# A graph-network kernel in three passes: the weight matrix of each source block built by a product, stored in pass 0 and read back in pass 1

## The reference

```python
src, dst = cat(src, arange(n)), cat(dst, arange(n))      # with self-loops
deg  = segment_sum(ew, dst);  dinv = rsqrt(deg)
conv = segment_sum((h @ W)[src] * (dinv[src] * ew * dinv[dst]), dst) + b
x = layernorm(x + sigmoid(conv(relu(conv(x, W1, b1)), W2, b2)))
z = x @ fc_w.T;  rh = edge_attr @ fc_r_w.T
e = leaky_relu(z[src] @ a0 + z[dst] @ a1 + rh @ a2)
alpha = softmax of e over the edges of one dst
x = layernorm(x + relu(segment_sum(alpha * (z[src] + rh), dst) + z @ loop_w))
```

## Time and profile before

| | us |
|---|---|
| median of three timed runs | 2405.95 |
| lowest and highest | 2403.78, 2406.47 |
| the profiled execution, first to last instruction | 3348.6 |
| PE busy | 2044.2 (61%) |
| DVE busy | 1834.8 (55%) |
| POOL busy | 1718.9 (51%) |
| ACT busy | 946.7 (28%) |

### The profile page before, as it was taken

How to read it: one execution, slowest core, us unless ns; L and a number is a source line. 1 busy time by engine, 2 the same in 40 slices (tenths; PEclk the granted TensorE clock), 3 DMA queues, 4 the chain that set the end, 5 groups by cost and what they waited for, 6 DMA issues and landing times.

```text
span 3348.6 us, 40819 instructions
## 1 busy us (share of the span) xinstructions
PE 2044.2 (61%) x13384; PEld 1762.3 (53%) x13384; DVE 1834.8 (55%) x7005; ACT 946.7 (28%) x1754; POOL 1718.9 (51%) x1781
## 2 busy tenths in 40 slices
PE   1416444588888911177777888106677667756786
PEld 1315433566767811166666677005666666645675
DVE  3626435577779810156656687217654564546457
ACT  1316000122233300033333444101254225412541
POOL 7351666665550067466556500555766646663640
PEclk9857667798999955588988899557778778877888
DMA  4112221222221122123333332525343534443431
GB/s 118 30 42 66 69 61 47 61 61 63 60 62 32 51 76 53 41 74 86 99 103 102 93 91 80 138 62 147 97 103 97 134 93 102 108 117 79 103 97 34
DMA packets 272093, 270.54 MB, mean 81 GB/s; under 512 B 43454, under 2 KB 218709, under 8 KB 271862
## 3 DMA queue, kind: packets, MB, share of 16 engines
q1 hardware_dynamic: 201790, 143.87, 15.1%
q0 software_dynamic: 56640, 117.52, 14.8%
q10 hardware_dynamic: 13448, 6.47, 0.7%
HBM read 254.14 MB, written 13.97 MB: 80 GB/s over the span
## 4 chain that ended last, share of the span: by engine, by line
PE 35%; DVE 21%; another core or an unknown queue 21%; issue 15%; ACT 4%; SPq 1%; DMA 1%; POOL 1%; ACTq 0%; DVEq 0%; POOLq 0%
PE ps L858 9%; PE ps L910 8%; DVE SR L1608 5%; PE ps L860 3%; PE ps L898 3%; PE ps L1045 2%; DVE U L1709 2%; DVE SR L1681 2%; DVE SR L1571 1%; PE ps L885 1%; DVE U L1648 1%; PE ps L1029 1%; POOL ring L720 1%; PE ps L792 1%
## 5 line engine op out<-in xcount | busy, mean ns | idle before, releaser
L720 POOL DMA_INDIRECT ring<-x_d,srcC x1132 | 1109.7, 980 | 971.2 <-issue 579.0
L858 PE MATMUL ps<-SR,ring 128*128 128x128 f32 x3540 | 672.5, 320 | 205.0 <-issue 132.0
L858 PEld LDWEIGHTS ps<-SR,ring 128*128 128x128 f32 x3540 | 580.5, 231 | 238.9 <-issue 178.9
L720 POOL DMA_INDIRECT ring<-h_d,srcC x494 | 469.9, 951 | 457.1 <-DMA h_d<-Lb 170.9
L1681 DVE TENSOR_SCALAR SR<-iota_r,cols 128x288 f32<-128x288 f32 x735 | 365.0, 564 | 303.9 <-remote 226.6
L910 PE MATMUL ps<-SR 128*128 128x288 f32 x1470 | 416.6, 435 | 118.1 <-ACT SR L1232 75.3
L910 PEld LDWEIGHTS ps<-SR 128*128 128x128 f32 x1470 | 292.3, 205 | 212.7 <-ACT SR L1232 77.5
L860 PE MATMUL ps<-SR 128*128 128x128 f32 x1564 | 340.3, 312 | 40.8 <-issue 34.6
L1232 ACT COPY SR<-ps 128x512 f32<-128x512 f32 (+1 forms) x195 | 106.0, 561 | 758.4 <-remote 502.9
L860 PEld LDWEIGHTS ps<-SR 128*128 128x128 f32 x1564 | 279.6, 228 | 48.3 <-issue 48.0
L898 PE MATMUL ps<-rows,SR 128*128 128x128 f32 x1470 | 196.2, 285 | 122.5 <-ACT SR L1241 90.6
(11 more groups left out here) (288 smaller groups left out, 2703.4 us busy)
## 6 DMA issues: line engine op xcount, KB each, us to landing
SR<-in_edge_attr_dram SPq DMA_DIRECT2D x97, 512.0 KB
SR<-low_d SPq DMA_DIRECT2D x90, 256.0 KB
U<-dlo_d SPq DMA_DIRECT2D x74, 256.0 KB
ring<-x_d,srcC POOLq DMA_INDIRECT x1132
ring<-h_d,srcC POOLq DMA_INDIRECT x494
SR<-dlo_d SPq DMA_DIRECT2D x12, 512.0 KB
ring<-in_edge_attr_dram SPq DMA_DIRECT2D x12, 512.0 KB
U<-lo_d SPq DMA_DIRECT2D x18, 256.0 KB
```

What stands on the lines that cost most here:

```text
L720: pool.indirect_dma_start(ring[:, ring_at(p, h if p < 2 else q), k, 0:width], None, (x if p == 0 and h < R0 else table)[:, :], bass.Indire ...
L858: last = nc.tensor.matmul(ps[(p * NA + k) % 2][:, at], ring[:, ring_at(p, h), j, 0:D], S[:, gg % NS, j, :], start=False, stop=stop)
```

## The change

The order of the two products is exchanged. Instead of looking up the rows of a block and multiplying them with the slot matrix, PE first multiplies one-hot and slot matrix of the block; that gives a 128 x 288 matrix with the weight of each source node at each destination (`build_pair`). ACT copies it to SBUF block by block (`copy_blocks`), and PE multiplies the block's rows with it (`sum_slots`). This matrix does not depend on the rows. In pass 0 SP stores the matrices of a chunk, 128 x 1152, in DRAM (`store_mat`); in pass 1 the six sets that pass 0 had also used are loaded from there (`load_mat`), and only the three others are built (`BUILT`). The one-hot is made from a column of low indices per block, with the node number along the free dimension, so its broadcast load is gone; the low indices are turned and stored only for the three sets of pass 2. The slot matrices have 11 buffers for 15, freed by the product. The matrices have three buffers in pass 0 and four in pass 1. In pass 1 the table gives built chunks more time than loaded ones (`EFFORT`). The rest of the diff renames semaphores of a path that these inputs do not take, and counters of pass 2.

```diff
-NL = -(-NB // 8)
-NQ = 15
+NQ = 11
+NBT = (3, 4)
+BCH = 4 * NARROW
 assert all(bank_of(t0) == bank_of(t0 + ST - 1) == k and column(t0) + SPAN <= BW for k, t0 in zip(SETK, SAT))
-CHUNK_AT = [[29 + m * 40 // (N0 * NC) for m in range(N0 * NC)], [1 + m * 57 // (len(USED[1]) * NC) for m in range(len(USED[1]) * NC)]]
+BUILT = [i for i in range(len(RUNS)) if i < N0 or RUNS[i] not in USED[0]]
+EFFORT = [4 if RUNS[N0 + m // NC] in USED[0] else 5 for m in range(len(USED[1]) * NC)]
+CHUNK_AT = [[29 + m * 40 // (N0 * NC) for m in range(N0 * NC)], [1 + sum(EFFORT[:m]) * 57 // sum(EFFORT) for m in range(len(USED[1]) * NC)]]
...
+def is_built(m):
+
+    return m // NC in BUILT
...
+def place_of(m):
+
+    return m % NBT[0] if m < N0 * NC else (m - N0 * NC) % NBT[1]
+
+
+def holder(m):
+
+    return m - NBT[0] if m < N0 * NC else m - NBT[1] if m - NBT[1] >= N0 * NC else None
...
-        ohS = part(2 * BW).rearrange("p (a n) -> p a n", a=2)
-        rowX = part(2 * BW).rearrange("p (a n) -> p a n", a=2)
-        loS = part(2 * BW).bitcast(BF16).rearrange("p (a n) -> p a n", a=2)
+        ohB = part(2 * BW).rearrange("p (a n) -> p a n", a=2)
+        mats = [part(BCH) for _ in range(NBT[0])]
...
+        slotL = s2C[:, 0:NSET * NB].rearrange("p (s a) -> p s a", a=NB)
...
+        mats.append(Lb[:, 2:5].rearrange("p a n -> p (a n)")[:, 0:BCH])
...
+            def store_mat(m):
+                sp.wait_ge(s("looked_copied"), slot_no(m, buckets(m)[-1]) + 1)
+                sp.dma_start(b_d[m, :, 0:len(buckets(m)) * NARROW], mat(m)).then_inc(mat_moved[place_of(m)], 16)
+
+            def load_mat(m):
+                if holder(m) is not None:
+                    sp.wait_ge(s("slot_summed"), slots_to(holder(m)))
+                sp.dma_start(mat(m), b_d[kept(m), :, 0:len(buckets(m)) * NARROW]).then_inc(mat_moved[place_of(m)], 16)
+
+            for m in range(N0 * NC):
+                store_mat(m)
...
+            await_mats_stored(sp)
+            for m in range(N0 * NC, N0 * NC + NBT[1]):
+                if not is_built(m):
+                    load_mat(m)
...
+                for m in range(N0 * NC + NBT[1], len(RUNS) * NC):
+                    if not is_built(m) and summed_at(holder(m)) == h:
+                        load_mat(m)
...
-            def look_up(m):
-                pe.wait_ge(s("oh_made"), m + 1)
-                if m >= 2:
-                    pe.wait_ge(s("looked_copied"), m - 1)
+            def build_pair(m, half):
+                for i, a in [*enumerate(buckets(m))][2 * half:2 * half + 2]:
+                    n = slot_no(m, a)
+                    if i == 0:
+                        pe.wait_ge(s("oh_made"), built_chunk(m) + 1)
+                    pe.wait_ge(s("slot_S"), n + 1)
+                    if n >= 2:
+                        pe.wait_ge(s("looked_copied"), n - 1)
+                    nc.tensor.matmul(ps[3 + n % 2][:, 0:NARROW], ohB[:, built_chunk(m) % 2, i * P:(i + 1) * P], slotS[:, n % NQ, :], start=True, stop=True
+                                     ).then_inc(s("looked"), 1)
+
+            def sum_slots(m):
+                if not is_built(m):
+                    pe.wait_ge(mat_moved[place_of(m)], 16 * moves_to(m))
                 for i, a in enumerate(buckets(m)):
-                    last = nc.tensor.matmul(ps[3 + m % 2][:, i * P:(i + 1) * P], ohS[:, m % 2, i * P:(i + 1) * P], rows[:, a, 0:D], start=True, stop=True)
-                last.then_inc(s("looked"), 1)
-
-            def sum_slots(m):
-                pe.wait_ge(s("looked_copied"), m + 1)
-                for i, a in enumerate(buckets(m)):
-                    n = m // NC * NB + a
                     if a == 0:
                         if m >= NC:
                             pe.wait_ge(s("set_copied"), m // NC)
                         clear(ps[5][:, :], P)
-                    pe.wait_ge(s("slot_S"), n + 1)
-                    nc.tensor.matmul(ps[5][:, SLACK:SPAN], rowX[:, m % 2, i * P:(i + 1) * P], slotS[:, n % NQ, :], start=False, stop=a == NB - 1
+                    if is_built(m):
+                        pe.wait_ge(s("looked_copied"), slot_no(m, a) + 1)
+                    nc.tensor.matmul(ps[5][:, SLACK:SPAN], rows[:, a, 0:D], mat(m)[:, i * NARROW:(i + 1) * NARROW], start=False, stop=a == NB - 1
                                      ).then_inc(s("slot_summed"), 1)
...
-                for m in chunks_at(0, h - 1):
-                    look_up(m)
+                pairs = [(m, half) for m in chunks_at(0, h - 1) for half in range(2)]
+                for m, half in pairs[:2]:
+                    build_pair(m, half)
                 for s_, g in made_at(h, 0):
                     count_before(s_, g)
                 for s_, g in made_at(h, 3):
-                    if g == ST // GT - 1:
+                    if g == ST // GT - 1 and s_ in XR:
                         turn_low(s_)
                 add_sets(0, h)
+                for m, half in pairs[2:]:
+                    build_pair(m, half)
                 sum_group(0, h)
...
-                for m in chunks_at(1, h - 1):
-                    look_up(m)
+                pairs = [(m, half) for m in chunks_at(1, h - 1) if is_built(m) for half in range(2)]
+                for m, half in pairs[:len(pairs) // 2]:
+                    build_pair(m, half)
                 for q in picks_at(h - 1):
                     pick(q)
                 add_sets(1, h)
+                for m, half in pairs[len(pairs) // 2:]:
+                    build_pair(m, half)
...
-            def copy_looked(m):
-                act.wait_ge(s("looked"), m + 1)
-                if m >= 2:
-                    act.wait_ge(s("slot_summed"), slots_to(m - 2))
-                n = len(buckets(m)) * P
-                nc.scalar.copy(rowX[:, m % 2, 0:n], ps[3 + m % 2][:, 0:n]).then_inc(s("looked_copied"), 1)
+            def copy_blocks(m):
+                for i, a in enumerate(buckets(m)):
+                    n = slot_no(m, a)
+                    if i == 0:
+                        if m == min(c for c in range(N0 * NC, len(RUNS) * NC) if is_built(c)):
+                            await_mats_stored(act)
+                        if holder(m) is not None:
+                            if holder(m) >= 0:
+                                act.wait_ge(s("slot_summed"), slots_to(holder(m)))
+                                if m < N0 * NC:
+                                    act.wait_ge(mat_moved[place_of(m)], 16 * (m // NBT[0]))
+                        else:
+                            act.wait_ge(s("slot_summed"), N0 * NB)
+                    act.wait_ge(s("looked"), n + 1)
+                    nc.scalar.copy(mat(m)[:, i * NARROW:(i + 1) * NARROW], ps[3 + n % 2][:, 0:NARROW]).then_inc(s("looked_copied"), 1)
...
-                n = m // NC * NL + m % NC // 2
-                c, w = m % NC % 2 * BW, len(buckets(m)) * P
-                act.wait_ge(low_loaded[n % 2], 16 * (n // 2 + 1))
-                if m >= 2:
-                    act.wait_ge(s("looked"), m - 1)
-                one_hot(ohS[:, m % 2, 0:w], loS[:, n % 2, c:c + w]).then_inc(s("oh_made"), 1)
+                c, s_ = built_chunk(m), RUNS[m // NC]
+                if m % NC == 0:
+                    act.wait_ge(s("unpacked"), s_ + 1)
+                if c >= 2:
+                    act.wait_ge(s("looked"), (c - 2) // NC * NB + buckets(c - 2)[-1] + 1)
+                for i, a in enumerate(buckets(m)):
+                    nc.scalar.activation(ohB[:, c % 2, i * P:(i + 1) * P], iota[:, :], ACT.Abs, bias=slotL[:, s_, a:a + 1]).then_inc(s("low_apart"), 1)
+                apart[0] += len(buckets(m))
+                act.wait_ge(s("low_apart"), apart[0])
+                w = len(buckets(m)) * P
+                nc.scalar.activation(ohB[:, c % 2, 0:w], ohB[:, c % 2, 0:w], ACT.Relu, bias=negp[:, 1:2], scale=-1.0).then_inc(s("oh_made"), 1)
...
+                if s_ in XR:
+                    v.tensor_copy(lowF, lowI)
+                v.tensor_scalar(slotL[:, s_, :], lowI, -1.0, None, ALU.mult).then_inc(s("unpacked"), 1)
...
-                        dve.wait_ge(s("slot_summed"), n - NQ + 1)
-                    v.tensor_scalar(slotS[:, n % NQ, :], iota_up, slotD[:, RUNS[i], a:a + 1], slotW[:, RUNS[i], a:a + 1], ALU.is_equal, ALU.mult
+                        dve.wait_ge(s("looked"), n - NQ + 1)
+                    v.tensor_scalar(slotS[:, n % NQ, :], iota_up, slotD[:, s_, a:a + 1], slotW[:, s_, a:a + 1], ALU.is_equal, ALU.mult
                                     ).then_inc(s("slot_S"), 1)
```

More of the change, by code:

```diff
@@ L140, in slots_to, with slot_no, built_chunk, kept @@
     return m // NC * NB + buckets(m)[-1] + 1
+def is_built(m):
+    return m // NC in BUILT
+def slot_no(m, a):
+    return BUILT.index(m // NC) * NB + a
+def built_chunk(m):
+    return BUILT.index(m // NC) * NC + m % NC
+def place_of(m):
+    return m % NBT[0] if m < N0 * NC else (m - N0 * NC) % NBT[1]
+def holder(m):
+    return m - NBT[0] if m < N0 * NC else m - NBT[1] if m - NBT[1] >= N0 * NC else None
```

(35 more changed lines are left out.)

103 lines of the change are left out of this document (47 added, 56 removed).

## The result

The kernel after takes 2463.86 us (median of four, 2459.69 to 2469.59), the kernel before in the same session 2406.21 (2403.78 to 2409.91): a ratio of 1.0242, interval 1.0217 to 1.0266. It is 58 us slower, where 35 were forecast; the direction and the range held, but one of the two terms did not. One of the later runs (of e6) took 4319 us and is left out.

What follows compares the result with a forecast made beforehand. PE was taken to bound passes 0 and 1, DVE close behind, with POOL's gathers next in pass 1. From the median of 2405.95 us, +72 in pass 0 and -36 in pass 1 gave 2441 us, range 2365 to 2510.

Steps and rivals of the forecast that it cites:

- Pass 0: Pass 0, held to be paced by PE: +72 us in all, with ends of +48 and +118.
- products against lookups: PE in pass 0: 0.513 us per product for 0.256 per lookup, over 294 blocks, +75.6 us.
- bank stall: Pass 0: ACT's copies out of two alternating PSUM banks limit products to 0.55 us each, +11 us; slow copies +39.
- The waits for the rank rows: Pass 0: PE's idle time waiting for DVE's rank rows shrinks as slot buffers free earlier, -18 us.
- The one-hot's +3: ACT in pass 0: the one-hot in four Abs parts is exposed 0.55 us at each of 6 sets, +3 us.
- the cycle "near 79 us for 68.7": Sign in a stretch of pass 0 without gathers: a cycle of six steps grows from 68.7 to near 79 us.
- "over 95%": Sign in a stretch of pass 0 without gathers: PE busy over 95% of the time.
- Pass 1: Pass 1 falls from PE's 599 us to POOL's 563, -36 us, with ends of -81 and 0.
- c: POOL's pace per gather in the timed runs, put between 0.944 and 1.25 us; 1.1 used, giving 543 us for pass 1.
- The saving on PE and DVE: Pass 1: PE's need falls from 599 to 548 us, by 28 of bare work and 23 of waits for S.
- Transfers bound the loaded steps: Rival, pass 1: matrix transfers at 284 GB/s make loaded steps 10.8 us, +70 us, 2511 in all; chance 0.17.
- Faster through decoupling: Rival, passes 0 and 1: PE's waits for DVE and S go wholly, gathers are quick, -33 us, 2373; chance 0.28.
- Covered by gathers: Rival: gathers pace pass 0, hiding its +72; c near 1.25, so pass 1 gains nothing, 2404; chance 0.09.

Runs made afterwards that it cites:

- e6: Kernel after with pass 0 products and ACT's copies (from the fourth chunk on) cut to 64 of 288 columns: 2419 to 2433 us over three runs, ratio 1.0091.
- second profile: Kernel before, unchanged, profiled again: span 2404.4 us, time 2406.24, without the unexplained waits that stretched the first profiled execution to 3348.6 us.
- e9: Kernel before with six of each eight gathers of pass 1 (374 for 494): 2381.07 us, ratio 0.9888; pass 1 lasts 627 us.
- e10: Kernel after with six of each eight gathers of pass 1: 2381.31 us, ratio 0.9897 to the kernel before; pass 1 lasts 569 us.
- e3: Kernel after with matrix stores and loads cut to 8 of up to 1152 columns per chunk, all waits kept: 2460.68 us, ratio 1.0228 to the kernel before.
- e8: Kernel before with the chunks of pass 0 spread over steps 25 to 68 in place of 29 to 68: 2388.47 us, ratio 0.9914.

## Why the prediction was right, and where it was not

**Pass 0, +72 forecast, +53 measured: right in its mechanism.** PE's added columns outrun what it gets back. By the terms: products against lookups were put at +75.6 and a bank stall of +11, and came to 103.1 of busy time and 13.1 of waits for copies. A product takes 0.609 us (179.1/294), not 0.55: it was priced by the mean of L910, whose matmuls stand in runs of eight products, while the new products mostly stand in runs of two (last section). The waits for the rank rows gave back 42.4 us, not 18, since the one clean cycle of the earlier trace rows held 4.2 (27 in 6.5 cycles) where the whole pass held 50.8. The 27.4 us that PE's other work lost stood in no term. The one-hot's +3 was fair: 2.2 more of waits (3.4 to 5.6). The costs were put too low and the gains too low as well, so the sum is nearer than its terms. In steps: the sums of the 31st and the 66th step begin at these times, before and after.

```profile
338.21 3.20 PE L858 MATMUL ps<-SR,ring 128*128 128x128 f32 x16
...
746.18 2.03 PE L858 MATMUL ps<-SR,ring 128*128 128x128 f32 x16
```

```profile
337.86 1.95 PE L909 MATMUL ps<-SR,ring 128*128 128x128 f32 x16
...
797.23 1.95 PE L909 MATMUL ps<-SR,ring 128*128 128x128 f32 x16
```

Six steps take 69.9 us before and 78.7 after (408.0 and 459.4 over 35, times six): the cycle "near 79 us for 68.7" that was to show it. PE was busy 94% of these 35 steps after the change (431.3 of 459.4 us), a little under the "over 95%".

**Pass 1, -36 forecast, -1 measured: this term failed,** in the step "So c lies between 0.944 and 1.25; I use 1.1". The usual distance is 1.25 and the mean 1.27, the end at which "POOL needs over 599 already". The row that told it was there: 129 gathers in 160 us, 1.24 each. The prediction set it aside because a sum for the timed runs gave 1.25 as the most that c could be. But that sum took two pauses, 83 and 108 us, from the stretched execution. In the second profile they are 43.3 and 48.9, the latter from the last start of a gather:

```profile
L720 POOL DMA_INDIRECT ring<-x_d,srcC x1132: 938/944/2447, 194.4 to 2355.5; - x189
```

With these, and the 24.5 us between passes 1 and 2, the same sum gives (2406 - 6 - 43.3 - 24.5 - 48.9)/1770 = 1.29, so it set no bound below the 1.24. The saving on PE and DVE was mis-sized by little: 51 us forecast (599 to 548), 58 measured (627 to 569 in e9 and e10). But the gathers take 625 us and the pause behind them 22 to 25, together the 649, so neither 627 nor 569 is seen.

**The rivals.** *Transfers bound the loaded steps:* no; e3 took them away and won 3 us, and the matrices moved at 366 GB/s, not at the 284 from the earlier trace rows. The Trainium skill (DMA: Bandwidth & Descriptors, section Bandwidth) has 341 GB/s for a load of 1 MB issued from GpSimd and would have struck this rival; the chunks here, at most 0.59 MB and issued from SP, moved a little faster, at the 366. PE waited for no matrix in pass 1; its waits for transfers between 869.5 and 1495 us are for gathers:

```profile
PE ps L843 <- DMA ring<-h_d,srcC: 46.0, 9, 15.5
PE ps L909 <- DMA ring<-h_d,srcC: 33.5, 14, 4.9
```

*Faster through decoupling:* the coupling did go, 42 us of waits in pass 0 and 22 of idle time in pass 1 (e9 and e10), but pass 1 could not use it, and the case had asked for c at 1.0 or less. *Covered by gathers:* half right. c is 1.25 and pass 1 gains nothing, as it says; but POOL runs ahead by up to 18 groups in the ring, so its pace covers PE only as long as PE needs no more than some 10 us for a step. PE needed 11.7 before (408.0/35) and 13.1 after (459.4/35), and the lag is paid at the end of the pass.

One error was 19 us too much for pass 0, the other a saving of 35 us in pass 1 that did not come. They have opposite signs, so the sum came within 23 us of the measured time in part by luck.

## What to carry to other kernels

A stage whose producer runs ahead through a ring ends with the backlog of its consumers, so read the tail between the producer's last piece and the next stage's first: here it held the whole difference, and starting the same work earlier and spreading it more thinly (e8) shortened it by 16 us. Price an issuing engine by the distance from start to start where nothing holds it, not by the duration of its instruction. Take pauses and rates from an execution that takes as long as the timed ones. And saved work in a stage that another engine paces is worth nothing until that engine has less to do, as e9 and e10 show.
